# A two-block MetaFormer with routed experts: the middle layer of the first expert loop handed on chunk by chunk, and the scan of the next weights cut into pieces

## What is computed

```python
x = x + L0_conv(ln_c(x));  t = to_tokens(x)
# first expert layer: 8 experts, 2 per token, middle width 512
h = einsum('nd,ehd->neh', ln_t(t), w1);  g = einsum('nd,ehd->neh', ln_t(t), w3)
eo = einsum('neh,edh->ned', silu(h) * g, w2);  t = t + einsum('ned,ne->nd', eo, comb)
x = from_tokens(t);  x = x + L1_conv(ln_c(x));  t = to_tokens(x)
# second expert layer: 8 experts, 2 per token, middle width 1024
for i in range(8):
    out = out + (silu(xf @ v1[i] + b1[i]) @ v2[i] + b2[i]) * comb[:, i:i + 1]
```

## Time and profile before

| what | us |
|---|---|
| median of 3 runs (lowest, highest) | 1333.01 (1328.87, 1334.24) |
| the profiled execution: its time, its span | 1335.55, 1333.8 |
| first products of the first loop begin | 364.6 |
| its last tile begins | 655.4 |
| the second block's first transpose on PE | 738.4 |

### The profile page before, as it was taken

The page is one execution under the profiler, slowest core; times in us unless marked ns, Lnnn a source line. Parts: engine busy times, 40 slices in busy tenths (PEclk is TensorE's granted clock), DMA queues, the critical chain, the costliest instruction groups (busy, mean ns, idle before and its releaser), DMA issues.

```text
span 1333.8 us, 25140 instructions
## 1 busy us (share of the span) xinstructions
PE 945.6 (71%) x7185; PEld 794.4 (60%) x7185; DVE 873.4 (65%) x1854; ACT 514.4 (39%) x983; POOL 442.6 (33%) x486
## 2 busy tenths in 40 slices
PE   5210577656399999999800668457999999999943
PEld 4100456515288888888700457416888888888842
DVE  6999789897444555555589886683555555555545
ACT  5200223276354444444433443283443333443312
POOL 1285000000045555555522560003444434444410
PEclk8655795558799999999955885557999999999975
DMA  7000007806633555455567312104222232222257
GB/s 229 1 0 0 0 1 224 280 0 201 227 88 94 155 154 155 99 154 158 152 214 241 126 63 77 50 0 103 72 79 71 77 78 75 75 75 75 75 165 252
DMA packets 169438, 147.22 MB, mean 110 GB/s; under 512 B 88432, under 2 KB 152376, under 8 KB 169272
## 3 DMA queue, kind: packets, MB, share of 16 engines
q1 hardware_dynamic: 151048, 103.76, 27.0%
q0 software_dynamic: 14000, 38.82, 9.1%
q10 hardware_dynamic: 4352, 4.20, 1.0%
HBM read 96.39 MB, written 30.93 MB: 95 GB/s over the span
## 4 chain that ended last, share of the span: by engine, by line
PE 57%; DVE 21%; issue 8%; DMA 6%; ACT 5%; SPq 1%; DVEq 1%; ACTq 0%; POOLq 0%; POOL 0%
PE bank L711 27%; PE bank L729 18%; PE bank L647 4%; PE bank L564 3%; DVE tok L1373 2%; DMA wreg<-rows_y 2%; DVE region L1032 2%; PE bank L764 2%; ACT xt L869 2%; DVE xt L1044 2%; DMA wreg<-in_L_ffn_w_dram 1%; PE bank L619 1%; DVE region L1031 1%; DVE region L1343 1%; PE bank L689 1%
## 5 line engine op out<-in xcount | busy, mean ns | idle before, releaser
L711 PE MATMUL bank<-xt,wreg 128*128 x3360 | 382.5, 274 | 30.9 <-DMA xt<-region 30.9
L711 PEld LDWEIGHTS bank<-xt,wreg 128*128 128x128 f16 x3360 | 330.7, 98 | 71.4 <-issue 31.3
L729 PE MATMUL bank<-wreg,region 128*128 128x256 f16 x2520 | 292.6, 273 | 16.2 <-DVE region L1347 15.1
L729 PEld LDWEIGHTS bank<-wreg,region 128*128 128x128 f16 x2520 | 243.6, 98 | 54.0 <-DVE region L1347 24.6
L891 ACT ACTIVATE region<-bank,b_t,fac 128x256 f32<-128x256 f32 x280 | 142.5, 560 | 226.3 <-PE bank L711 215.7
L495 POOL DMA_INDIRECT rows_y<-region,put_now x140 | 138.4, 988 | 221.4 <-DVE region L1358 140.3
L455 POOL DMA_INDIRECT region<-rows_x,fetch_now x144 | 144.4, 1003 | 185.8 <-DMA xt<-region 94.0
L1343 DVE SCALAR_TENSOR_TENSOR region<-bank,fac,region 128x256 f32<-128x256 f32 x140 | 61.2, 479 | 157.8 <-PE bank L711 106.7
L564 PE MATMUL bank<-ident,xn 128*128 128x128 f32 x256 | 56.6, 383 | 112.6 <-DVE xn L1003 104.4
L1350 DVE TENSOR_SCALAR region<-region,fac 128x512 f16<-128x512 f32 x140 | 76.5, 546 | 69.3 <-ACT region L891 64.2
L564 PEld LDWEIGHTS bank<-ident,xn 128*128 128x128 f32 x256 | 45.8, 208 | 121.3 <-DVE xn L1003 110.6
(11 more groups left out here) (237 smaller groups left out, 1238.7 us busy)
## 6 DMA issues: line engine op xcount, KB each, us to landing
wreg<-in_L_ffn_w_dram SPq DMA_DIRECT2D x48, 512.0 KB, 5.9
wreg<-in_L_ffn_w_dram SPq DMA_DIRECT2D x16, 1024.0 KB
wreg<-rows_y SPq DMA_DIRECT2D x48, 256.0 KB, 3.6
region<-in_L_ffn_w_dram SPq DMA_DIRECT2D x12, 1024.0 KB, 7.4
rows_x<-region SPq DMA_DIRECT2D x16, 512.0 KB, 3.2
wreg<-in_x_dram SPq DMA_DIRECT2D x4, 1024.0 KB, 9.4
out_dram<-xt ACTq DMA_DIRECT2D x16, 256.0 KB, 3.6
xt<-region SPq DMA_TRANSPOSE x148
```

The costliest lines, as they stand in the source:

```text
L711: last = pe.matmul(to, w[:, e, k, ws_, c * P:(c + 1) * P], x_cols[:, bass.ds(b, 1), :, xs_, k, :].rearrange("p j r n -> p (j r) n"), start ...
L729: last = pe.matmul(yb[:, r * C:(r + 1) * C], lhs[:, c, r * P:(r + 1) * P], w[:, e, c, ws_, :], start=first, stop=end, skip_group_check=True)
```

## The change

Four things, all in or around the first expert loop.

1. **Middle layer by chunks.** `up` goes chunk by chunk: 6 matmuls of w1 and 6 of w3 into the two halves of one bank, then `z_ready` is raised (four times per tile as before, but now each time for a complete chunk). ACT makes silu of 256 columns four times instead of 512 columns twice. DVE waits for each silu by itself. `down` starts each chunk with its four matmuls of the high half, behind `hi_ready`, and then the two of the low half behind `lo_ready`.
2. **The scan in pieces.** `load_scan` is gone. `load_piece(n)`, by SP, once per tile, loads 1/32 of all of `v1` and of `v2` (256 KB each, 512 columns per partition) into one of two slots in `region`; DVE reduces each piece (1024 elements per partition) at the end of every tile. Tiles beyond 32 read the first pieces again. `peaks1` then joins the pieces.
3. **Experts 0 and 1 of the next layer** are loaded by ACT's queue (`load_ahead`, four DMAs of 1 MB) into the place where the scan's slots were, once `w_lo[0]` is complete and before ACT reads `bounds`.
4. **SP ahead of and behind the loop.** SP no longer waits for `w_lo[0]` and has no loads there: it goes from the last weight load to `bounds` and to the turns of tiles 0 and 1, then loads piece 0. Behind the loop it waits for `peaks_found` and for the last piece, then as before for the transposes and the scatters.

The core of the diff:

```diff
+            def load_piece(n):
+                for m in range(2):
+                    row = n * P if isinstance(n, int) else (n % PIECES) * P
+                    slot = n if isinstance(n, int) else n % 2
+                    sp.dma_start(piece1[:, bass.ds(slot, 1), m, :].rearrange("p j n -> p (j n)"),
+                                 blocks[m][bass.ds(row, P), :]).then_inc(piece_loaded, 16)
...
                     with sp.Fori(edges[e], edges[e + 1]) as n:
                         sp.wait_ge(z_ready[f], 4 * n + 4)
                         turn_rows(f, n + 2)
-                    if f == 0 and 1 <= e < E - 1:
-                        sp.wait_ge(scanned, e)
-                        load_scan(e + 1)
+                        if f == 0:
+                            with sp.Fori(n, n + 1) as m:
+                                sp.wait_ge(piece_loaded, 32 * m + 32)
+                            with sp.Fori(n, n + 1) as m:
+                                sp.wait_ge(scanned, m)
+                            load_piece(n + 1)
...
-            for r in range(2):
-                sp.wait_ge(xc_ready[r][0], 16 * total + 32)
-            sp.wait_ge(y_free[0], 32 * total + 16)
+            sp.wait_ge(peaks_found, 1)
+            for waited, each, more in ((piece_loaded, 32, 32), (xc_ready[0][0], 16, 32), (xc_ready[1][0], 16, 32), (y_free[0], 32, 16)):
+                with sp.Fori(total, total + 1) as m:
+                    sp.wait_ge(waited, each * m + more)
...
-                    for r in range(2):
-                        for hs, ws_ in PARTS:
-                            lhs = (hid_hi, hid_lo)[hs]
+                    for hs in range(2):
+                        if f == 0 and hs == 1:
+                            pe.wait_ge(lo_ready[0], 2 * halves * tile + c + 1)
+                        lhs = (hid_hi, hid_lo)[hs]
+                        for r, ws_ in ((0, 0), (0, 1), (1, 0), (1, 1)) if hs == 0 else ((0, 0), (1, 0)):
...
+            def scan1_peaks(n):
+
+                with dve.Fori(n, n + 1) as m:
+                    dve.wait_ge(piece_loaded, 32 * m + 32)
+                dve.tensor_reduce(peak_piece[:, :, bass.ds(n % PIECES, 1)].rearrange("p m a -> p (m a)"),
+                                  piece1[:, bass.ds(n % 2, 1)].rearrange("p j m n -> p (j m) n"), AX.X, ALU.max,
+                                  apply_absolute_value=True).then_inc(scanned, 1)
```

More of the change, by code:

```diff
@@ L227, in stage1_of @@
         def stage1_of(e):
-            return scan1[:, 1 - e] if e < 2 else stage1[:, e % 2]
+            return ahead1[:, e] if e < 2 else stage1[:, e % 2]
         def image_rows(v):
@@ L346, in _ @@
                     load_stage0(2 * i + j, j, stage_loaded[0])
-            sp.wait_ge(w_lo[0], 6 * E)
-            for e in range(2):
-                load_scan(e)
             def turn_rows(f, n):
@@ L363, in turn_tiles @@
                 turn_rows(f, 1)
+                if f == 0:
+                    load_piece(0)
                 for e in range(E):
@@ L703, in up @@
             def up(f, e, h, b):
-                ws = ((w1_s, zb[2 * (h % 2)]), (w3_s, zb[2 * (h % 2) + 1])) if f == 0 else ((v1_s, zb[h]),)
-                for w, z in ws:
-                    for c in (2 * h, 2 * h + 1):
-                        to = z[:, (c % 2) * TILE:(c % 2 + 1) * TILE]
+                ws = (w1_s, w3_s) if f == 0 else (v1_s,)
+                for c in (2 * h, 2 * h + 1):
+                    for m, w in enumerate(ws):
+                        z, at = (zb[c], m) if f == 0 else (zb[h], c % 2)
+                        to = z[:, at * TILE:(at + 1) * TILE]
                         for k in range(KC):
@@ L870, in route, with load_ahead @@
                                        scale=id_f[:, b % 2, bass.ds(4 * i + b // 2, 1)]).then_inc(ids_listed, 1)
+            def load_ahead(e):
+                act.dma_start(ahead1[:, e, 0].rearrange("p (c h) -> p c h", c=KC),
+                              v1[e].rearrange("(c p) h -> p c h", p=P)).then_inc(ahead_loaded, 16)
+                act.dma_start(ahead1[:, e, 1].rearrange("p (c d) -> p c d", c=8),
+                              v2[e].rearrange("(c p) d -> p c d", p=P)).then_inc(ahead_loaded, 16)
             def experts(f):
                 halves = FH[f] // (2 * P)
+                if f == 0:
+                    act.wait_ge(w_lo[0], 6 * E)
+                    for e in range(2):
+                        load_ahead(e)
                 edges = [act.value_load(bounds[0:1, e:e + 1], min_val=0, max_val=TILES) for e in range(E + 1)]
@@ L879, in experts @@
                             if f == 0:
-                                act.wait_ge(z_ready[0], 2 * halves * n + 2 * h + 1)
-                                act.activation(gate_act[:, h], zb[2 * h][:], ACT.Silu, scale=fac[:, 0, e:e + 1]
-                                               ).then_inc(silu_done[f], 1)
+                                for c in (2 * h, 2 * h + 1):
+                                    act.wait_ge(z_ready[0], 2 * halves * n + c + 1)
+                                    act.activation(gate_act[:, h, (c % 2) * TILE:(c % 2 + 1) * TILE], zb[c][:, 0:TILE], ACT.Silu,
+                                                   scale=fac[:, 0, e:e + 1]).then_inc(silu_done[f], 1)
                                 for c in (2 * h, 2 * h + 1):
@@ L916, in high1 @@
             def high1(e, m):
-                if m == 0 and e >= 2:
+                if m == 0 and e < 2:
+                    act.wait_ge(ahead_loaded, 64)
+                elif m == 0:
                     act.wait_ge(stage_loaded[1][e % 2], 32 * (e // 2))
```

52 lines of the change are left out of this document (28 added, 24 removed).

## The result

The changed kernel takes 1322.02 us, median of five runs (1319.95 to 1327.92), against 1333.01 us for the kernel before in its five runs beside it. The ratio is 0.9923, with an interval of 0.9895 to 0.9950. So it is faster, by 11.0 us, where 20.6 were forecast: little more than half of the forecast gain came. The time lies above the forecast's own range (1306 to 1318) and inside the wide one (1304 to 1330), which took in the rivals. The profiled execution has a span of 1326.2 and is the slowest of the five.

What follows compares the result with a forecast made beforehand. PE was taken to bound the first loop, with a 0.63 us hole per tile. The terms -7.5 - 0.2 - 15.3 - 0.5 + 2.9 = -20.6 gave a median of 1312.4 us, range 1306 to 1318, with rivals 1304 to 1330.

Steps and rivals of the forecast that it cites:

- start: Ahead of the first loop: SP no longer waits for split weights, so the first product comes 7.5 us earlier, at 357.1.
- first tile: First tile of the first expert loop: it loses only its smaller hole, 0.2 us.
- 33 periods: Tiles 1 to 34 of the first loop: period 8.05 us against 8.51, 15.3 us saved.
- last tile and tail: End of the first loop and behind it: last tile gains 0.5 us, SP's later loads cost 2.9.
- The chain of chunk 3: End of a tile's middle layer: silu, product and halves after the last signal; high half ready at 7.0 us, low at 7.5.
- in time: In `down`: chunk 3's halves, wanted by PE at 7.2 and 7.65 us, are ready 0.15 to 0.2 early.
- 0.17 that the forecast added for a late signal: Allowance per tile for a late last signal and the tight place at chunk 2's low half: 7.88 becomes 8.05 us.
- A: Rival, first loop: jitter vanishes with the 2 MB bursts, 7.88 us per tile, another 5.6 less, 1306.8; chance 0.12.
- B: Rival, first loop: the feed of rows by POOL takes over, slowed by the pieces; 1317.4 to 1328.2 us; chance 0.20.
- C: Rival, first loop: turns queue behind the pieces on SP, period 8.9 us, kernel slower at 1341; chance 0.08.
- D: Rival, loop start: PE or first rows are held otherwise, so the 7.5 us are not gained, 1320; chance 0.08.

Runs made afterwards that it cites:

- e9: Kernel before with SP's turns of tiles 0 and 1 moved ahead of its wait for the split weights; 1327.18 us, ratio 0.9951.
- e1: The changed kernel run again, unaltered; 1323.03 us, ratio 0.9939 to the kernel before.
- e5: The kernel before run again, unaltered, for a second profile; 1333.78 us, ratio 1.0005.
- e4: Changed kernel with six further, already satisfied waits on PE behind each tile's last matmul in the first loop; 1335.29 us, ratio 1.0027.
- e3: Changed kernel, but all six of chunk 3's matmuls in `down` wait for its low half; 1325.20 us, ratio 0.9957.
- e2: Changed kernel with silu started behind the w1 part of each chunk, adding two waits in `up`; 1318.51 us, ratio 0.9901.
- e8: Changed kernel with SP's wait for the last piece moved behind the first output loads; 1322.35 us, ratio 0.9920.
- e10: Changed kernel with the next piece's loads ahead of the turns in SP's iteration; 1322.40 us, ratio 0.9930.
- e11: Kernel before, bursts kept, with early turns of tiles 0 and 1, chunks passed on singly and silu behind w1; 1319.95 us, ratio 0.9902.

## Why the prediction was wrong

By its own steps, with the means of the five profiles of the kernel before and the three of the changed one:

| step | forecast | measured | from |
|---|---|---|---|
| start | -7.5 | -7.4 | A: 14.9 to 7.5; e9 alone has it |
| first tile | -0.2 | -0.2 | 10.4 to 10.2, within a spread of over 1 us |
| 33 periods | -15.3 | -3.7 | 8.27 (without the first profile) to 8.16 |
| last tile and tail | +2.4 | +3.3 | T: 82.0 to 85.3 |
| sum | -20.6 | -8.0 | by the medians: -11.0 and, in e1's session, -8.8 |

**Start: right.** Mechanism and size. The first profile seemed to contradict it (364.62 to 361.86) until the first product was read from the end of the weight splits and not from the span's start.

**The tile: wrong, and this is the step that failed.** Of its 15.3 us, 3.7 came. It has two errors, of 8.0 and 3.6 us. The larger one is its base. "The 33 periods [...] take 280.9, 8.51 each" was true of the one execution and not of the kernel: four further profiles have 8.265 to 8.274, and 33 x (8.51 - 8.27) = 8 us of the forecast gain were not there to be had in them. Whether some of the timed executions have such late signals is not known; their cause stays open. The sign was in the earlier trace rows: tile 19 took 8.21, a value that four other periods of the 33 have to the hundredth and none undercuts. It is the length of the undisturbed tile, as e5 shows it: low half of chunk 2 done at 6.83, its matmuls from 6.89 on, 12 of them in 1.32. I took jitter that the change does not touch for part of what it would remove.

The smaller error is the end of the tile, 8.16 instead of 8.05. The chain of chunk 3 came out as worked out, 7.37 instead of 7.5, and PE's need for its low half at 7.65 as well. But "in time" for the matmul is not in time for the sequencer: it needs another 0.75 us for the loop's turn, and when that wait ended the array had only 0.5 us of matmuls left (7.88 - 7.37). The period is the last wait plus that turn, 7.37 + 0.78 = 8.15, and not 7.88. In the kernel before, the turn was hidden: chunk 3's low half was done at 7.23 (in e5), and nearly 1 us of matmuls still lay ahead. e4 (each wait on top counts in full), e3 (four more matmuls behind the wait cost 0.04 us) and e2 (a low half 0.5 earlier gives 7.86) show it from three sides. Of the 0.17 that the forecast added for a late signal nothing was needed.

**Tail: the size right within 1 us, the cause half wrong.** SP's loads did go out at 17. But the forecast laid the cost on SP's wait for the landing; by e8 taking that wait away gains nothing that can be told from the spread, and by e10 it is the piece ahead of the outputs in the queue.

**The rivals.** A (jitter vanishes with the bursts) has the wrong cause: e5, with bursts, has none. B (the feed takes over) did not occur at 8.15: the turns slipped late in the loop without moving the period. At 7.86 it is real in e11, and late pieces cost time in e2, there by the new waits in `up`. Its rule, cited there from the Trainium skill (Trainium Kernel Development and Optimization, Key Constraints), that all queues share the engines, agrees with e11: POOL's fetch took 6.06 us to land beside SP's burst, against a median of 2.9 in the tiles ahead, and PE waited 2.52 for its rows. C did not occur. D seemed to and did not: the distance A is 7.5 in all three profiles of the changed kernel.

## What to carry to other kernels

Before a gain is worked out from a mean period, look at how the periods are spread: the value that returns to the hundredth is the kernel, the rest may be the execution, and a second profile of the kernel before is worth more than a finer sum on the first. A loop on a fast engine ends not when its last wait is satisfied and its last matmuls are done, but a loop turn after that wait: have at least that much work queued behind it, or make the last signal earlier. And measure a stage from the event ahead of it, not from the start of the execution, where unchanged stages differ by several us from one execution to the next.

## What the runs showed of the hardware

A turn of a loop with bounds in registers takes PE's sequencer 0.7 to 0.8 us from its last satisfied wait to the next weight load, though its instructions show only 0.29 us; a satisfied wait costs 0.056 us (e4). The granted clock differs between executions in stages that use PE lightly: 0.88 and 0.77 in the weight turns of two profiles of one and the same kernel (43.6 and 50.0 us, of which PE's busy time explains 2.45), and in the second block's convolution 0.89 with 57.3 us (e5) and 0.83 with 61.9 (e10). A load issued 0.8 us earlier behind 512 KB in its queue landed 0.2 earlier (e8 against e1, one profile each). A fetch by POOL beside a 2 MB burst of SP took 6.06 us to land instead of 2.9 (e11). A maximum over 1024 elements takes 1.22 us on DVE, a quarter of the 4.41 for 4096 with 0.12 on top.
